# A two-layer graph attention network on one core: four stretches of the instruction order changed around TensorE's waits

## The reference, cut to what matters

```python
def gat_layer(x, W, a_s, a_d, b, edge_index, concat):
    n = x.shape[0]; H, C = a_s.shape
    h = (x @ W).reshape(n, H, C)
    src, dst = edge_index
    alpha_s = jnp.einsum('nhc,hc->nh', h, a_s)
    alpha_d = jnp.einsum('nhc,hc->nh', h, a_d)
    e = jax.nn.leaky_relu(alpha_s[src] + alpha_d[dst], 0.2)
    m = segment_max(e, dst)
    e = jnp.exp(e - m[dst])
    alpha = e / (segment_sum(e, dst)[dst] + 1e-16)
    out = segment_sum(h[src] * alpha[:, :, None], dst)
    return out.reshape(n, H * C) + b
h = elu(gat_layer(x, W1, ...))          # 8 heads of 768: (512, 6144)
out = gat_layer(h, W2, ...)             # 1 head: (512, 768)
return layernorm(x + out)
```

## Time and profile before

| | us |
|---|---|
| median of 3 runs | 663.96 (663.59 to 666.13) |
| profiled execution | 667.82, span 666.0 |
| PE busy | 642.9 (97%) |
| DVE / ACT / POOL busy | 510.6 (77%) / 334.0 (50%) / 208.1 (31%) |
| mean granted TensorE clock | 0.99 |
| PE waits, O L1180 for ACT L L445 / for DVE L L747 | 1.8 / 1.6 |
| PE waits, R L1147 for DVE y L780 (twice, the longest 1.4) | 2.3 |
| PE waits, O L1294 for DVE hl L942 | 2.0 |
| PE waits, R L1120 for ACT gh L463 / R L1122 for DVE gl L868 | 0.8 / 0.5 |
| DVE hl L707, four low parts of head 2, from 224.00 | 3.56 |
| DVE dn L947 and L949, from 650.08 to 650.48 | 0.4 |

### The profile page before, as it was taken

One profiled execution on the slowest core, in us unless ns is written; L12 is line 12 of the kernel. 1 busy time (PEld: TensorE's weight loads), 2 busy tenths in 40 slices (PEclk: granted clock), 3 DMA queues, 4 the chain that ended last, 5 costly groups with the idle time before them and its releaser, 6 DMA issues.

```text
span 666.0 us, 9320 instructions
## 1 busy us (share of the span) xinstructions
PE 642.9 (97%) x3437; PEld 552.4 (83%) x3446; DVE 510.6 (77%) x927; ACT 334.0 (50%) x560; POOL 208.1 (31%) x121
## 2 busy tenths in 40 slices
PE   6999999999799999999999999999999999989986
PEld 4765567989688878988899889988998899868875
DVE  7899996798877977576956685677876788789466
ACT  6698972535614734454444444454436344613362
POOL 0000000131543460257224822473157415631120
PEclk9999999999899999999999999999999999998989
DMA  8413421115051620134112320324043404400002
GB/s 309 151 49 95 143 72 48 48 48 190 28 162 56 220 81 1 47 96 132 60 46 76 104 108 24 95 64 151 25 139 105 136 25 139 170 24 1 1 0 95
DMA packets 22173, 59.36 MB, mean 89 GB/s; under 512 B 2544, under 2 KB 2800, under 8 KB 22128
## 3 DMA queue, kind: packets, MB, share of 16 engines
q1 hardware_dynamic: 22128, 58.76, 27.2%
HBM read 54.03 MB, written 4.72 MB: 88 GB/s over the span
## 4 chain that ended last, share of the span: by engine, by line
PE 58%; DVE 5%; ACT 2%; issue 1%; ACTq 0%
PE O L1180 21%; PE R L1075 6%; PE R L1081 6%; PE R L1078 6%; PE R L1153 5%; PE R L1150 5%; PE R L1147 5%; PE R L1097 1%; DVE junk L809 1%; PE R L1264 1%; DVE L L753 1%; DVE res L962 1%; PE O L1294 1%; PE O L1297 1%; PE O L1291 0%
## 5 line engine op out<-in xcount | busy, mean ns | idle before, releaser
L1009 POOL TENSOR_TENSOR W2l<-Wr,W2h 128x768 fp32r<-128x768 f32 x48 | 97.5, 2035 | 219.6 <-ACT W2h L404 219.5
L1013 POOL TENSOR_TENSOR Pl<-L,Ph 128x512 fp32r<-128x512 f32 x34 | 53.5, 1582 | 178.3 <-ACT Ph L453 178.3
L1075 PE MATMUL R<-W1h,xTh 128*128 128x384 f32 x312 | 106.4, 341 | 0.0
L1078 PE MATMUL R<-W1l,xTh 128*128 128x384 f32 x312 | 105.3, 338 | 0.0
L1081 PE MATMUL R<-W1h,xTl 128*128 128x384 f32 x312 | 105.3, 338 | 0.0
L682 DVE CUSTOM_DVE_ANT_0 junk<-h,abc 128x768 bf16<-128x768 f32 x64 | 64.5, 1008 | 48.3 <-ACT h L416 46.8
L1180 PE MATMUL O<-W2h,gh 128*128 128x512 f32 (+1 forms) x384 | 80.4, 345 | 3.5 <-ACT L L445 1.8
L1180 PE MATMUL O<-W2l,gh 128*128 128x512 f32 (+1 forms) x384 | 78.1, 340 | 0.0
L1180 PE MATMUL O<-W2h,gl 128*128 128x512 f32 (+1 forms) x384 | 76.9, 336 | 0.0
L416 ACT COPY h<-R 128x384 f32<-128x384 f32 x62 | 29.5, 478 | 82.5 <-PE R L1081 76.5
L1092 PE MATMUL O<-ohd,ohs 128*128 128x512 bf16 x255 | 62.3, 391 | 8.7 <-DVE ohs L648 6.2
(11 more groups left out here) (170 smaller groups left out, 1197.5 us busy)
## 6 DMA issues: line engine op xcount, KB each, us to landing
Wr<-in_W SPq DMA_DIRECT2D x101, 384.0 KB, 3.2
abc<-in_as SPq DMA_DIRECT2D x9, 384.0 KB, 4.4
abc<-in_ad SPq DMA_DIRECT2D x9, 384.0 KB, 5.8
h_rows<-h SPq DMA_DIRECT2D x8, 384.0 KB, 2.3
hl<-h_rows SPq DMA_DIRECT2D x8, 384.0 KB, 5.5
xin<-in_xT SPq DMA_DIRECT2D x6, 256.0 KB, 5.9
xr<-in_x SPq DMA_DIRECT2D x1, 1536.0 KB, 6.8
out<-res SPq DMA_DIRECT2D x4, 384.0 KB, 2.3
```

What stands on the lines that cost most here:

```text
L1009: e.tensor_tensor(W2l[:, m % N2, :], Wr[:, n, :], W2h[:, m % N2, :].bitcast(f32), ALU.subtract).then_inc(s_w2l, 1)
L1013: e.tensor_tensor(Pl[:, t, d0:d1], L[:, t, d0:d1], Ph[:, t, d0:d1].bitcast(f32), ALU.subtract).then_inc(s_Pl, 1)
L1075: e.matmul(bank[:, 0:HALF], xTh[:, f, xs], hi[:, ws], start=f == 0, stop=False)
L1078: e.matmul(bank[:, 0:HALF], xTh[:, f, xs], lo[:, ws], start=False, stop=False)
```

## The change

Four edits, all of order. (1) ScalarE and VectorE, head 2: the scores and the sums of P come before the high and low parts of h; one of W2's high parts moves in between the steps of the scores. (2) Layer 2: the partial sums of P, their sum, and the low parts of h change places on VectorE (`h < H` takes them out of `scores`). (3) `stage_C` of head 0: blocks 0 and 1 are each called in two parts, by groups, and count s_C in the second. (4) `denominators(7)` is called in block 4 of C(6, ·) instead of block 5, and `tail_denominators` after all of d = 0 and 1.

```diff
@@ scalar_program, high parts and scores of head 2
                 if h == 2:
+                    high_w2(1, 4)
+                    scaled_as(2, 24)
+                    scores(2, 2, 0, NT, ring_bank("r2", 2, 0), (gl_value(1, FT - 1), (s_g, 2 * FT)), 8, lambda u: high_w2(1, 5) if u == 3 else None)
+                    high_sums(2)
                     for t in range(NT):
                         high_h(2, t)
-                    high_w2(1, 4)
-                    high_w2(1, 5)
-                    scaled_as(2, 24)
-                    scores(2, 2, 0, NT, ring_bank("r2", 2, 0), (gl_value(1, FT - 1), (s_g, 2 * FT)), 8)
-                    high_sums(2)
@@ vector_program, scores
-                        if u in (2, 4):
+                        if h < H and u in (2, 4):
@@ vector_program, head 2
                 if h == 2:
+                    scores(2, 2, 0, NT, ring_bank("r1", 2, 0), 9)
+                    sums_P(2)
                     for t in range(NT):
                         low_h(2, t)
-                    scores(2, 2, 0, NT, ring_bank("r1", 2, 0), 9)
-                    sums_P(2)
@@ vector_program, layer 2
-            e.wait_ge(s_sd, 3 * H + 2)
-            e.tensor_tensor(y2[:, :], y2[:, :], rb[:, :], ALU.add).then_inc(s_sd, 1)
             for t in range(NT):
                 e.wait_ge(s_hh, NT * H + t + 1)
                 e.tensor_tensor(hl[:, t, :], res[:, t, :], hh[:, t, :].bitcast(f32), ALU.subtract).then_inc(s_hl8, 1)
+            e.wait_ge(s_P, NT * H + NT)
+            for i, to in enumerate((y2, rb)):
+                e.tensor_tensor(to[:, :], L[:, 2 * i, :], L[:, 2 * i + 1, :], ALU.add).then_inc(s_sd, 1)
+            e.wait_ge(s_sd, 3 * H + 2)
+            e.tensor_tensor(y2[:, :], y2[:, :], rb[:, :], ALU.add).then_inc(s_sd, 1)
@@ tensor_program, stage_C
-            def stage_C(h, c, groups=range(6), between=None):
+            def stage_C(h, c, groups=range(6), between=None, ends=True):
...
-                mm.then_inc(s_C, 1)
+                if ends:
+                    mm.then_inc(s_C, 1)
@@ tensor_program, heads 1 to 7
-                for c in range(FT):
-                    stage_C(h - 1, c, between=(lambda h=h: denominators(h)) if c == FT - 1 else None)
+                if h == 1:
+
+                    for c in range(2):
+                        stage_C(0, c, groups=range(4), ends=False)
+                    for c in range(2):
+                        stage_C(0, c, groups=(4, 5))
+                for c in range(2 if h == 1 else 0, FT):
+                    stage_C(h - 1, c, between=(lambda h=h: denominators(h)) if c == (FT - 2 if h == H - 1 else FT - 1) else None)
@@ tensor_program, stage D
             for t in range(NT):
-                if t == NT - 1:
-                    tail_denominators()
                 for d in range(2):
                     for i in range(2):
                         stage_D(d, t, i)
+            tail_denominators()
```

## The result

The changed kernel takes 659.3 us (median of 5, 658.9 to 660.2); measured beside it, the kernel before took 666.13 (median of 5, 663.6 to 669.5): ratio 0.989, 95% interval 0.985 to 0.993, so about 7.4 us less by the ratio and 6.8 us by the two medians. Measured once more in a later group of runs it was 0.990 (0.987 to 0.994). The kernel before varies from execution to execution with the mean clock that TensorE was granted over it: on one chip 31 executions took 664.2 us at 0.995 (one), 665.1 to 667.4 at 0.990 to 0.992 (17), and 668.9 to 670.7 at 0.985 to 0.989 (13). Spells at half clock (stretches of a few us in which the granted clock is 0.50) come in some executions of the same code and not in others.

A forecast was written before the change was run, and what follows sets the result against it. TensorE, busy 97%, was taken as the bound until the last stage, where VectorE and ScalarE set the end. Gains 1.4 + 0.3 + 0.75 + 2.2 = 4.65 us off the median 663.96 gave 659.3 us, range 656.6 to 662.0.

The forecast's parts named there:

- Part 1: Head 0's first two projection blocks, O2/O3 pieces last: waits go, gain 1.4 us, bounds 0 and 4.1.
- the case with two collisions: Head 1: GpSimd collides twice with VectorE's low parts of h, which end at 191.5; gain at A(1,1) 2.6 us.
- the case of three: Head 1: three such collisions, low parts of h end at 193.3; gain at A(1,1) only 0.8 us.
- 4.1 to 4.4: Transposes of head 2's source terms: TensorE waits 1.1 us for sums, leaving 4.1 to 4.4 of 5.5 us.
- Part 4: Last stage, low parts before sums, denominators after d = 0 and 1: gain 2.2 us, bounds 1.2 and 2.6.
- Part 2: Head 2's scores first: 1.7 us wait goes, about 1.3 returns at A(2,1); gain 0.3 us, from -0.6 to 1.4.
- Part 3: Head 7's denominators in block 4: new 1.1 us wait, A(7,3) sooner; gain 0.75 us, bounds 0.4 and 1.0.
- A: Rival: heads 0 to 2 give everything back through VectorE's queue and collisions; 661.0 us, chance 0.20.
- B: Rival: VectorE and GpSimd collisions fall between the steps; 655.5 us, chance 0.08.
- C: Rival: TensorE's clock falls after the new waits, making it slower; 666.4 us, chance 0.06.
- D: Rival: head 0's reordering frees nothing, O2's and O3's pieces wait anyway; chance under 1 in 100.
- Its own range: Forecast time's spread, from 0.3 to 2.6 in head 0, -0.6 to 1.4 in head 2, rest +-0.5: 657.2 to 661.4 us.

The follow-up runs named there:

- later gate: Changed kernel, GpSimd's W2 low parts held until r12 ends, head 7's denominators ahead of block 5, layer 2's ahead of t = 3: 654.3 us, 0.981.
- part 2 alone: Kernel before with only head 2's scores and sums of P ahead of the high and low parts of h: ratio 0.998.
- part 1 alone: Kernel before with only blocks 0 and 1 of head 0's projection split into two calls each: ratio 0.994.
- part 3 alone: Kernel before with only head 7's denominators moved ahead of the last pass of block 4: ratio 0.996.

## Why the prediction was right, and where it was off

- **Part 1, "I take 1.4 us": right mechanism, term too small.** 2.88 us less 0.13 in the next stretch; the case with two collisions ("2.6 us") is what happened. The 1.4 was a compromise with the case of three, which "some 0.3 us" decided; in the trace the fifth GpSimd operation starts 0.09 us after the last low part had taken its place, and 0.07 to 0.09 us after it in five other traces with the split and no gate. The foreseen wait at the transposes (1.1) was 1.02. That collisions take the rest is shown: without them the stretch is 29.91 us (later gate), 4.2 us less than before, inside the "4.1 to 4.4" of the working.
- **Missed: the length of a spell is not fixed.** The terms of parts 1 and 4 were read from one profile and then taken off a median of other executions, with the words "the gains are waits at full clock"; but part 4's 2.2 has a spell in it, and so has part 1's 5.5. The first block's stretch varies over 1.3 us with the same code, the wait for hl was followed by a spell in two of the five traces that have it, and the same kernel's mean clock lies anywhere from 0.985 to 0.995. Part 4's 2.2 (measured 2.08) is 0.54 for the two moves together (2.3 won by the low parts, 1.8 lost by the denominators) and 1.55 for the spell.
- **Part 2, "I take 0.3 us": 0.72 us** (0.87 with the next stretch), within its bounds. The sums were ready at the upper end of the working (238.07 in the times of the kernel before, in the changed kernel and in part 2 alone; forecast 237.3 to 238.1), and no GpSimd operation held up the low parts (3.55 us). The reciprocal then ended at 244.8 instead of 245.1, since successive operations overlap a little in the records. The working itself leaves 0.45 us (245.55 less 245.1), of which 0.3 was taken. The new wait was 0.88, not 1.3.
- **Part 3, 0.75 us: 0.70.** The denominators' place lengthened stage C by 1.15, forecast 1.1. That the same denominators one pass later, between blocks 4 and 5, lose nothing, I did not look for.
- **Part 4, "the residual chain allows only 2.2": right that TensorE's 4 us do not reach the end**, shown by TensorE being done 4 us sooner and the end 2.08. But the chain's length (8.60 us) is only half of the reason: its start hung on the denominators, which the change itself had put late. With them back the same chain starts 1.8 us sooner.
- **Rivals.** A (heads 0 to 2 give all back) and B (no collisions) fall by the first stretches. C (the clock falls after the new waits) falls: the clock is 1.00 from 192 to 200, and over the whole of 165.6 to 606.8, in which the new waits of 1.02, 0.90 and 0.88 us lie. D falls: no wait on O2 or O3.
- **The sum.** 4.65 forecast, 6.4 in the stretches, 6.8 by the medians, about 7.4 by the ratio. That the time came out exact is luck: the low median and the low gain cancelled. So what is confirmed is the four mechanisms, with terms 1 and 2 at half of what was measured or less, and not the 659.3. "Its own range", 657.2 to 661.4, is also narrower than its bounds give when they are added (656.5 to 661.8).

## What to carry to other kernels

When a wait of the bounding engine goes, follow the other engine's queue behind the next two or three fixed points: here VectorE took back half of 5.5 us, and a gate on GpSimd won 1.3 us of it. Work that GpSimd does as early as it can may cost the bounding chain more than its lateness would: here it is better placed beside operations that it does not hold up (the maxima, the reciprocal) than beside VectorE's two-input ones. Move one thing at a time where two moves serve one wait: of part 4's two, one won 2.3 us and the other lost 1.8. And read the size of a clock spell from several profiles, since the same wait costs another amount each time.

## What the runs showed of the hardware

- VectorE operations on 128 x 4 values (0.16 us alone) took 0.91 and 1.77 us beside GpSimd's low parts, and 0.16 again once these were moved: a small operation waits until the other is done, the second of them for nearly the whole of a GpSimd operation (1.77 of 1.85 us). The maxima, with one operand in PSUM, did not wait (0.69 us either way). The Trainium skill (SBUF — State Buffer, Who interferes with whom) puts the contention down to VectorE's two SBUF inputs; the runs agree, and show that size gives no exemption. That the one that issued first holds the pair for its whole instruction the section says of VectorE's two-port modes; here it is seen for two-input operations.
- The scatter goes with the half-clock spells: within one kernel the time falls into groups by the mean granted clock, as in part 1 alone (661.2 and 661.4 us at 0.999 and 1.00; 662.2 and 662.3 at 0.995; six of 665.2 to 665.6 at 0.990).
- The same idle time of TensorE is not always followed by the lower clock: after 2.04 us the clock was 0.64 in the kernel before and 1.00 in part 3 alone. With 1.84 + 1.61 us a spell came in all five traces, one to two passes long. After waits of up to 1.39 us none came.
- A spell needs no idle time before it: late in head 7's projection TensorE runs 24 matmuls of two columns, twice, without a wait. At eight of the 28 such places in the fourteen traces a spell began, from 0.4 us before their end to 1.6 us after it (0.51 over 606.8 to 609.5 in the changed kernel), and each cost 1.6 us. Why at these eight, the runs do not show.
